# Attention edge stages of a graph network: masks and lines held in SBUF, target places spread over the partitions by TensorE instead of by broadcast loads

## The reference

```
h   = (x @ W).reshape(n, 4, 64)
a_s = einsum('nhc,hc->nh', h, att_src);  a_d = einsum('nhc,hc->nh', h, att_dst)
e   = leaky_relu(a_s[src] + a_d[dst], 0.2)
m   = segment_max(e, dst);  ex = exp(e - m[dst]);  denom = segment_sum(ex, dst)
out = segment_sum(h[src] * (ex / denom[dst]), dst) + b
```

## Time and profile before

| | |
|---|---|
| Median of 3 runs | 5089.54 us |
| Profiled execution, its span | 5091.65 us, 5089.7 us |
| The two `gat_edges` phases | 1953 to 3390, 3524 to 4970 us |
| POOL busy | 2936.1 us (58%) |
| VectorE busy | 3127.1 us (61%) |
| TensorE multiplying | 3447.0 us (68%) |
| Mean granted clock of TensorE | 0.785 of 2.4 GHz |

### The profile page before, as it was taken

The page is one execution under the profiler, slowest core; times in us unless marked ns, Lnnn a source line. Parts: engine busy times, 40 slices in busy tenths (PEclk is TensorE's granted clock), DMA queues, the critical chain, the costliest instruction groups (busy, mean ns, idle before and its releaser), DMA issues. The chain is left out here.

```text
span 5089.7 us, 75249 instructions
## 1 busy us (share of the span) xinstructions
PE 3447.0 (68%) x14837; PEld 2133.0 (42%) x14837; DVE 3127.1 (61%) x8081; ACT 2517.7 (49%) x7710; POOL 2936.1 (58%) x3014
## 2 busy tenths in 40 slices
PE   1698999999889873566666665655466666666660
PEld 1444444444444562444444444443244444444450
DVE  4888788888878663454454454567345454454468
ACT  1588888888888521343343343343233333333342
POOL 2265566656555204566666666636566666666646
PEclk7899999999999986676676766678577676677675
DMA  3332232323222224344444444424344444444425
GB/s 109 124 87 81 82 87 86 87 85 88 81 85 81 77 83 126 109 118 120 124 119 120 125 119 120 125 54 136 103 115 123 125 118 120 125 119 120 125 72 154
DMA packets 274535, 541.37 MB, mean 106 GB/s; under 512 B 73060, under 2 KB 161887, under 8 KB 274144
## 3 DMA queue, kind: packets, MB, share of 16 engines
q0 software_dynamic: 134912, 376.36, 27.3%
q1 hardware_dynamic: 132212, 154.29, 9.5%
q10 hardware_dynamic: 7020, 6.40, 0.4%
HBM read 495.47 MB, written 41.31 MB: 105 GB/s over the span
## 5 line engine op out<-in xcount | busy, mean ns | idle before, releaser
L1084 POOL DMA_INDIRECT arena<-h_rows,idx x1856 | 1860.1, 1002 | 1183.4 <-issue 479.6
L1228 PE MATMUL ps<-arena,z 128*128 128x264 f32 x3712 | 1420.9, 534 | 118.0 <-issue 88.4
L681 POOL DMA_INDIRECT arena<-y_rows,idx x928 | 890.8, 960 | 775.9 <-ACT arena L712 369.7
L1342 DVE TENSOR_TENSOR z<-ps,z 128x264 f32 x928 | 397.5, 428 | 1229.0 <-remote 529.5
L1148 ACT ACTIVATE z<-z 128x256 f32<-128x256 f32 x928 | 378.9, 408 | 1556.9 <-remote 960.1
L1228 PEld LDWEIGHTS ps<-arena,z 128*128 128x128 f32 x3712 | 907.7, 262 | 331.9 <-issue 118.6
L755 PE MATMUL ps<-arena 128*128 128x512 f32 x1856 | 911.1, 614 | 94.0 <-DVE z L809 77.1
L1199 PE MATMUL ps<-z 128*128 x5568 | 393.1, 178 | 836.8 <-issue 596.3
L710 ACT ACTIVATE arena<-arena 128x128 f32<-128x128 f32 x2784 | 907.2, 392 | 8.1 <-issue 4.2
L1199 PEld LDWEIGHTS ps<-z 128*128 128x128 bf16 x5568 | 330.1, 107 | 1060.5 <-issue 996.2
L1140 ACT ACTIVATE z<-iota,dst_x 128x128 f32<-128x128 f32 x1856 | 641.3, 393 | 24.5
(11 more groups left out here) (224 smaller groups left out, 3007.3 us busy)
## 6 DMA issues: line engine op xcount, KB each, us to landing
z<-lo_rows SPq DMA_DIRECT2D x116, 512.0 KB
arena<-h_rows,idx POOLq DMA_INDIRECT x1856
arena<-y_rows,idx POOLq DMA_INDIRECT x928
z<-seg_rows SPq DMA_DIRECT2D x232, 64.0 KB
h_rows<-arena SPq DMA_DIRECT2D x98, 132.0 KB, 1.7
arena<-h_rows SPq DMA_DIRECT2D x98, 132.0 KB, 2.3
res_rows<-z SPq DMA_DIRECT2D x98, 128.0 KB, 1.7
arena<-res_rows SPq DMA_DIRECT2D x98, 128.0 KB, 2.1
```

What stands on the lines that cost most here:

```text
L681: pool.indirect_dma_start(out=ring[:, r, :], out_offset=None, in_=s.y_rows, in_offset=bass.IndirectOffsetOnAxis(ap=rows_of[:, u, n:n + 1], ...
L1084: pool.indirect_dma_start(out=ring[:, u * SCORED + n, :], out_offset=None, in_=h_rows, in_offset=bass.IndirectOffsetOnAxis(ap=s.idx[:, u, ...
L1228: last = t.matmul(ps[:, bank[q % 4], 0:ROW], sel[:, q % SELS, k, :], ring[:, u * SCORED + 2 * q + k, :], start=(k == 0), stop=(k == 1))
L1342: v.tensor_tensor(dst, ps[:, bank[q % 4], 0:ROW], dst, ALU.add).then_inc(z_ok, 1)
```

## The change

Setup stores only two things for these phases: a mask of 130 bf16 values for each slot (`mask_rows`, 0 or -1e30, read forward as one mask and backward as the other) and the six lines in bf16. `gat_edges` loads all of it at its start, for all groups, and SP issues nothing after that: places as they stand (256 KB, 8 slots of 128 bf16 values on a partition), masks to 4 x 32 partitions, lines as one broadcast. For every 4 slots TensorE multiplies a column of the identity, read 128 times, with 512 columns of the places (`spread`), which puts one row on all partitions of a PSUM bank. VectorE makes the one-hots from there, in 8 pieces of 512 values for each group instead of 2 of 2048, 5 pieces ahead of the group. The two element-wise steps of `maxima` become two scans, and the segments' second pair of masks is no longer needed.

```diff
# setup
-        s.seg_rows = dram("seg_rows", (SLOT_COLS, 4 * P))
-        s.line_rows = dram("line_rows", (SLOT_COLS // SCORED, 6 * SCORED))
+        s.mask_rows = dram("mask_rows", (SCORED, SLOT_COLS // SCORED, MASK), BF16)
+        s.line_rows = dram("line_rows", (SLOT_COLS // SCORED, 6 * SCORED), BF16)
...
-            for n in range(4):
-                sp.dma_start(s.seg_rows[:, n * P:(n + 1) * P]..., seg[:, n, :, :]).then_inc(put, 16)
+            for n in range(P // SCORED):
+                sp.dma_start(by_quarter[n], mask[n * SCORED:(n + 1) * SCORED, :, :]).then_inc(put, 16)
...
# gat_edges, sync engine
-            def load(g, u):
-                for i in range(2):
-                    ...sp.wait_ge(hot_ok, (g - 1) * 2 + i + 1)
-                    sp.dma_start(lo_bc[:, i, :], lo_lines[...].broadcast_to([P, HALF * P])).then_inc(lo_in[i], 16)
-                for h in range(HEADS):
-                    sp.dma_start(seg[h * SCORED:(h + 1) * SCORED, u, :, :], s.seg_rows[...]).then_inc(seg_in[u], 16)
-                sp.dma_start(lin[:, u, :, :], s.line_rows[bass.ds(g, 1), :].broadcast_to(...)).then_inc(lin_in[u], 16)
-            run_all(SCORED_GROUPS, 2, load)
+            sp.dma_start(lo, s.lo_rows.rearrange("(c p k) e -> p c (k e)", p=P, k=4)).then_inc(lo_in, 16)
+            for h in range(HEADS):
+                sp.dma_start(mask[h * SCORED:(h + 1) * SCORED, :, :], s.mask_rows[:, 0:SCORED_GROUPS, :]).then_inc(mask_in, 16)
+            sp.dma_start(lin..., s.line_rows[0:SCORED_GROUPS, :]....broadcast_to([P, SCORED_GROUPS * 6 * SCORED])).then_inc(lin_in, 16)
...
# gat_edges, TensorE
+            def spread(g, j):
+                n = g * PIECES + j
+                if n >= 2:
+                    pe.wait_ge(hot_ok, n - 1)
+                t.matmul(ps[:, 4 + n % 2, :], ident_b[:, n % P:n % P + 1].broadcast_to([P, P]), lo[:, n // P, :], start=True, stop=True).then_inc(bc_ok, 1)
...
                     collect(g, u, q)
+                    if q % 2 == 0:
+                        ahead, j = divmod(q // 2 + 6, PIECES)
+                        if g + 1 + ahead <= last_group:
+                            spread(g + 1 + ahead, j)
...
-            for q in range(STEPS_IN):
-                look_up(0, 0, q)
+            for j in range(2):
+                spread(0, j)
+            for j in range(PIECES):
+                look_up(0, 0, 2 * j)
+                look_up(0, 0, 2 * j + 1)
+                if j + 2 < PIECES:
+                    spread(0, j + 2)
             source(0)
             maxima(0)
+            for j in range(6):
+                spread(1, j)
...
# gat_edges, VectorE
-            def one_hot(g, i):
-                dve.wait_ge(lo_in[i], g * 16 + 16)
-                    dve.wait_ge(look_ok, (g - 1) * STEPS_IN + (i + 1) * (STEPS_IN // 2))
-                v.tensor_scalar(hot[:, i, :], lo_bc[:, i, :], s.p_f[:, :], None, ALU.is_equal).then_inc(hot_ok, 1)
+            def one_hot(g, j):
+                dve.wait_ge(bc_ok, g * PIECES + j + 1)
+                    dve.wait_ge(look_ok, (g - 1) * STEPS_IN + 2 * j + 2)
+                v.tensor_scalar(hot[:, j * 4 * P:(j + 1) * 4 * P], ps[:, 4 + (g * PIECES + j) % 2, :], s.p_f[:, :], None, ALU.is_equal).then_inc(hot_ok, 1)
...
             def maxima(g, u):
-                chain(v.scalar_tensor_tensor(seg_m, seg[:, u, 2, :], linesT[:, 0, 0:1], run_b, ALU.add, ALU.max))
-                v.scalar_tensor_tensor(seg_max, seg[:, u, 3, :], linesT[:, 1, 0:1], seg_m, ALU.add, ALU.max).then_inc(max_ok, 1)
+                v.tensor_tensor_scan(run_f[:, ::-1], mask[:, g, 0:P], scT, linesT[:, 0, 0:1], ALU.add, ALU.max).then_inc(scan_ok, 1)
+                dve.wait_ge(scan_ok, g + 1)
+                v.tensor_tensor_scan(seg_max[:, ::-1], mask[:, g, P:0:-1], run_f, linesT[:, 1, 0:1], ALU.add, ALU.max).then_inc(max_ok, 1)
...
                         message(g + 1, 1 - u, q + 2 - STEPS_IN)
+                    if q % 2 == 0:
+                        ahead, j = divmod(q // 2 + 5, PIECES)
+                        if g + 1 + ahead <= last_group:
+                            one_hot(g + 1 + ahead, j)
...
-                        n = {0: 0, 2: 1}.get(q)
-                        if n is not None:
-                            one_hot(g + 1, n)
...
-            for i in range(2):
-                one_hot(0, i)
+            v.tensor_copy(ident_b, s.ident[:, :]).then_inc(ident_ok, 1)
+            for j in range(PIECES):
+                one_hot(0, j)
...             (the clearing of the sums follows here, before and after)
+            dve.wait_ge(mask_in, 16 * HEADS)
+            dve.wait_ge(lin_in, 16)
...
             for q in range(2):
                 message(0, 0, q)
+            for j in range(5):
+                one_hot(1, j)
```

More of the change, by code:

```diff
@@ L38 @@
 BIG = 1e30
+MASK = P + 2
 assert BLOCKS % 7 == 0 and SLOTS % (2 * GROUP) == 0 and TILES < ROWS and SLOTS % SCORED == 0
@@ L251, in setup @@
     last = part(SLOT_COLS, F32, by_e)
-    seg = part(4 * SLOT_COLS).rearrange("p (t c e) -> p t c e", t=4, e=P)
-    fwd, bwd, npre, npost = (seg[:, n, :, :] for n in range(4))
+    npre = part(SLOT_COLS, F32, by_e)
+    mask = part(SLOT_CHUNKS * MASK // 2, BF16, ("p (c e) -> p c e", dict(e=MASK)))
+    lines_b = part(6 * P // 2, BF16, ("p (t e) -> p t e", dict(t=6)))
     reps = part(6 * 4 * P)
@@ L415, in _ @@
             v.memset(by_s(B)[:, :, SCORED - 1:SCORED], -BIG)
-            v.memset(by_s(D)[:, :, SCORED - 1:SCORED], -BIG).then_inc(rep_ok, 1)
+            step(v.memset(by_s(D)[:, :, SCORED - 1:SCORED], -BIG))
+            v.tensor_copy(lines_b[q8, :, :], base6[q8, :, :]).then_inc(rep_ok, 1)
             dve.wait_ge(next_t, 1)
@@ L1031, in gat_edges @@
         ("abs_ok", "sel_ok", "msg_ok", "agg_ok", "z_ok", "dve_step", "up_ok"))
-    seg_in, lin_in, lo_in = ([s.sem(n) for _ in range(2)] for n in ("seg_in", "lin_in", "lo_in"))
+    mask_in, lin_in, lo_in, bc_ok, ident_ok = (s.sem(n) for n in ("mask_in", "lin_in", "lo_in", "bc_ok", "ident_ok"))
     turns = [(SCORED_GROUPS + 1 - u) // 2 for u in range(2)]
@@ L1045, in gat_edges @@
     away = part(2 * 2 * P).rearrange("p (b k n) -> p b k n", b=2, k=2)
-    hot = part(HALF * P, BF16).rearrange("p (u e) -> p u e", u=2)
-    lo_bc = part(HALF * P, BF16).rearrange("p (u e) -> p u e", u=2)
-    seg = part(2 * 4 * P).rearrange("p (u t e) -> p u t e", u=2, t=4)
+    hot = part(SCORED * P // 2, BF16)
+    lo = part(SLOT_COLS // 2, BF16).rearrange("p (c e) -> p c e", e=4 * P)
+    ident_b = part(P // 2, BF16)
+    mask = part(SCORED_GROUPS * MASK // 2, BF16).rearrange("p (g e) -> p g e", e=MASK)
     parts = part(BLOCKS * 8 * PARTS // 2, BF16).rearrange("p (k q n) -> p k q n", q=PARTS, n=8)
@@ L1054, in gat_edges @@
     w3 = part(3 * P).rearrange("p (t n) -> p t n", t=3)
-    ad, seg_m, seg_max, diff, rise = (part(P) for _ in range(5))
+    ad, seg_max, diff, rise = (part(P) for _ in range(4))
     runs = part(2 * P).rearrange("p (t n) -> p t n", t=2)
```

53 lines of the change are left out of this document (19 added, 34 removed).

## The result

The changed kernel takes 5135.19 us (median of 19 runs), the kernel before took 5108.34 us on the same chip (19 runs): ratio 1.0061, 95% interval 1.0046 to 1.0076. That is no change by the bound of 1%, on the slower side. The profiled execution took 5117.7 us (span 5115.6), that of before 5091.65 us.

What follows compares the result with a forecast made beforehand. POOL's gathers were taken to be near the bound, with some 6 us of waiting a group. On 5091.65, +59 us for 56 groups and +16 for two phase starts gave 5167; forecast 5165 us, range 4950 to 5270.

Steps and rivals of the forecast that it cites:

- the rival that gave 5116, the added work hides: Steady groups: POOL's pauses take in one-hots and spreads, only chain and start remain, 5116 us, no difference; chance 0.18.
- The loads are worth little: Steady group: nobody waits for the removed loads to speak of; gain taken as 0.3 us, between 0 and 6.
- One-hots, +0.5 us a group: VectorE, steady group: eight one-hots from PSUM at 0.68 us replace two of 0.77; cost 0.5 us, ends 0 and 1.3.
- spreads, +0.7: TensorE, steady group: eight spreads of 0.35 us; four stand where TensorE sets the pace, 1.4 us, half of it counted.
- The term of 59 us: All steady groups: the sum of +1.05 us a group, times 56, gives +59 us.
- The waits for one-hots bring nothing: TensorE, steady groups: 233.6 us in 47 waits for one-hots go, but the period stays; gain taken as 0.
- Start, +8 us a phase: Start of each phase: group 0's one-hots hang on slow look-ups, clearing of the sums behind; +8 us, ends 0 and +15.
- Setup, 0 to -3: Setup: some VectorE work and 2 MB of stores fewer, beside gathers and small stores; 0, at most -3 us.
- The crawl's cause: Slow stretch of TensorE and VectorE late in POOL's long gather runs, about 9 of 15 us lost; not from loads.
- The sign announced for it: Last 10 us of each long POOL run, without loads: VectorE under 0.3 busy and single look-up multiplications.
- The port rival: VectorE's fast one-hot from SBUF holds POOL's gathers back; freed, 0.5 us a group, 5139 us; chance 0.04.
- Nothing hides: Steady groups: all added work of one-hots, spreads and scans counts, +4.25 us a group, 5346 us with the start; chance 0.12.

Runs made afterwards that it cites:

- b_noloads: Kernel before, with the loads of lines and masks cut to those of group 0 (output not the reference's): ratio 0.9982 to the kernel before.
- a_clear: Changed kernel, with VectorE clearing the sums before the eight one-hots of group 0 instead of after them: ratio 1.0030 to the kernel before.
- a_again: Changed kernel, nothing edited, run on a chip of the second (faster) sort: 4541 us, ratio 1.0076 to the kernel before.
- a_hold: Changed kernel, with POOL waiting before slot 8 of group 0 until that group's 16 look-ups are done: ratio 1.0001 to the kernel before.
- b_hold: Kernel before, with POOL waiting before slot 8 of group 0 until its 16 look-ups are done, on the second sort of chip: ratio 1.0053.
- a_spread2: Changed kernel, with each of the 464 spreads issued twice, on the second sort of chip: ratio 1.0073 to the kernel before.

## Why the prediction was right, and where it was not

The time, 5135 us in the median and 5117.7 profiled, against 5167 by the sum, lies in the range, but the forecast's own case was "slower" (chance 0.43), and what came is "within 1%" (0.33). It is close to the rival that gave 5116, the added work hides; that the numbers agree so well is partly luck, for the start cost twice what this rival has for it.

- *The loads are worth little.* Right: b_noloads, -9 us with an interval from -22 to +4. The reading that decided it, the start of the phase in the earlier trace rows, was sound.
- *One-hots, +0.5 us a group; spreads, +0.7.* Sizes: 745 ns against 0.68 us assumed, 445 ns against 0.35. Cost: the groups between group 1's copy and the end took 1281.6 us in the first phase (1456.2 - 147.9 - 26.7, the last being from group 28's copy to the last addition) and 1279.8 before; in the second they are equal within 0.3 us. The term of 59 us measured 2. That is the step that failed: "where TensorE sets the pace" was taken for a cost, and the period does not follow TensorE's work.
- *The waits for one-hots bring nothing.* Right as far as the period goes. TensorE still waits for them.
- *Start, +8 us a phase.* The mechanism was right: spreads between crawling look-ups, the last one-hots at 2035 and 2038, the clearing behind them (at 2041.52). The size was 17.3 and 14.9, the end of the range for it. The first scan comes 14.6 and 12.2 us later after the first gather than before; 5.6 and 3.3 of that are look-ups that end later (3 forecast), and 9.0 and 8.9 are the clearing, of which the sum had 3. The clearing was thus the term most under-priced, and a_clear, which is 10.2 and 6.6 us a phase shorter, bears it out. VectorE stood idle 34.98 and 25.88 us between one-hots of group 0.
- *Setup, 0 to -3.* Right: it ends 2.8 us sooner. The other 5 us by which the first phase began sooner are the convolution's and chance.
- *The crawl's cause.* "When POOL has issued for more than some 10 us without a pause" is not sufficient: a_again's POOL issues through a whole group, and no sequencer is slow. It takes such a run *and* a chip of the first sort. There the look-ups do crawl because POOL issues (a_hold). What in those chips makes it, and what sets the period of 47.7 to 47.9 us there, stays open: the period was the same without loads, with 4 us more of VectorE's and 3.6 us more of TensorE's work a group, and with POOL's own work 1.5 us longer or 1.5 us shorter. A cycle of TensorE, VectorE and POOL that the crawl stretches until POOL must stop would do that, but this is argued, not shown.
- *Late semaphores, overlooked.* On the chips with the crawl a semaphore can come long after the multiplication that gives it. In the changed kernel the spread for one-hot 3 (counted from 0) has its record's end 9.57 us after the first gather, its semaphore update is recorded at 27.00, and the one-hot starts at 27.03; in a_again the three stand at 9.58, 9.60 and 9.62. The end of a multiplication is modelled, the start of the one-hot is not. The look-ups' next updates stand at 24.9, 43.8 and 59.9, 16 to 19 us apart, where the kernel before has three look-ups that end 16.8 us apart: so the pace in the crawl is about the same, and the forecast "again near 6 multiplications in 16 us" held, though the windows look empty.
- *A rival that nobody tested: the recording.* Each run on record lists a span and a granted clock beside its time, so none is known to have run without a profile. The traces of the two sorts of chip are not equally complete: 31,600 to 32,800 semaphore updates in each of the eight of the first sort, 75,800 to 81,300 in the four of full kernels on the second; 296 spreads with a record against 464. It may be that on the slower chips the writing of records holds the engines, and that the crawl and the longer time belong to profiled executions; a_hold would fit this too, since each gather of POOL's ends with 16 updates of a semaphore. No run decides it. It also warns of the labels: "remote" stands before 315.8 us of idle time of the changed kernel's additions, and in a_again, whose records are whole, 815.4 of 824.8 us are put down to the collects.
- *The sign announced for it was badly chosen.* VectorE under 0.3 busy over 15 us: the changed kernel has such stretches only about 2073 (0.29) and 3987 us (0.26), while the lowest of a usual group is 0.36; before it was 0.27. So the sign came, but not in each long run as announced, and a slightly different kernel would have spoken for the loads, which b_noloads rules out. VectorE's share is as low as 0.17 in a_again, without any crawl, where it waits for gathers. The sequencer's own instructions are the better sign.
- *The port rival* had the right mechanism and the wrong sum. The Trainium skill (SBUF — State Buffer, section "Who interferes with whom") says that a VectorE instruction in a two-port mode locks GpSimd out. The traces agree for the old one-hot out of SBUF (in b_hold 55 gathers begin under one, mean 1049 ns). The same section says that a `tensor_tensor` has no such mode and, with both inputs in SBUF, contends only with a GpSimd instruction that reads SBUF, so that it did not stall DMAs. The message is a `tensor_tensor`, and here the traces differ from the page: the gather at 2119.32 takes 1.45 us, 0.50 more than usual, with 0.63 of a message left. The measurement decides. The message was overlooked in the prediction. Where POOL is the bound, the change made it worse, since more gathers begin under a message (493 against 355).
- *Nothing hides* is out by the period, 0.13 us longer where this rival had 4.25; on the second sort of chip a_spread2 says the same of TensorE's work.

## What to carry to other kernels

Before a term is summed over all turns of a loop, ask whether the period follows that engine at all: here work was added on two engines and the loop did not move, while the start, where nothing overlaps, took twice its price. Whatever hangs behind the last link of a serial start (a memset of 10.8 us) is to be issued before it. Where GpSimd's gathers are the bound, look at what VectorE runs when each of them begins; one operand in PSUM was enough to end the hold. And count windows from an event of the phase, not from the start of the span: a phase that begins 8 us sooner made the same windows show different work.

## What the runs showed of the hardware

- Two sorts of Trainium2 chip differ by 12.7% on the same program: the kernel before took 5078 to 5108 us (four medians) and 4509 to 4511 (two). The convolution's edge phase, which no edit touches, shows it too: its gathers take 1494 to 1519 us on the one and 1308 to 1309 on the other. All of this is of runs that list a profile's span. On the slower ones register and semaphore instructions of 0.6 to 0.8 us stand in the traces while POOL issues indirect DMAs, and semaphores come late; on the others there are hardly any. The mean granted clock of TensorE is lower on the slower ones, 0.78 to 0.79 against 0.83 to 0.84 for the kernel before and 0.81 to 0.82 against 0.83 to 0.84 for the changed one; whether that is a cause or comes of TensorE's idle time is not shown. The usual durations are the same on both (the register load's median 303 ns). The Trainium skill (Advanced Engine Details and Errata, section "Clock Domains") describes power profiles in which all sequencers and datapaths are slower; equal medians speak against that here.
- A change can cost the same 0.6 to 0.8% on both for unlike reasons: the start of the phases on one, POOL's stretched gathers on the other.
- Gathers are not bound by their transfer: in the first phase the last packet of each ends in the median 2.5 us after the gather's beginning, at the end of a run of 64 and in the steady state alike, on both sorts of chip. Beside loads it takes longer, in the first 12 us up to 5.2 us in the kernel before and 8.2 in the changed one (packets taken in order, 48 a gather).
- More work for VectorE made the kernel faster by 50 us on the second sort of chip: with it 311 gathers begin under a message instead of 493, and the gathers are 51 us shorter.
